# A DLRM-style recommender on one core: four late tables in two chunks instead of eight in four, in the last step

## The chip, the cores and the metric

The kernel runs on one core of one Trainium2 chip. The metric is the time on the device of one execution, in microseconds, taken by the median of several runs. All arithmetic is in float32.

## The reference

The batch has 2048 samples, each with 13 dense features and one index into each of 26 tables of 12,500 rows of 64 floats.

```python
x = relu(dense @ Wb0 + bb0)          # 13 -> 512
x = relu(x @ Wb1 + bb1)              # -> 256
d = relu(x @ Wb2 + bb2)              # -> 64
sp = emb[arange(26)[None, :], sparse_idx]
T = concatenate([sp, d[:, None, :]], axis=1)      # 27 vectors of 64 per sample
Z = einsum('bnd,bmd->bnm', T, T)
inter = Z[:, li, lj]                 # the 351 pairs below the diagonal
h = concatenate([d, inter], axis=1)
h = relu(h @ Wt0 + bt0)              # 415 -> 512
h = relu(h @ Wt1 + bt1)              # -> 256
p = sigmoid(h @ Wt2 + bt2)
```

## The kernel before, in words

The batch is worked off in 8 steps of 256 samples. A step is 128 columns `c` with two samples (halves `h`) each, and it is taken in two units `u` of 64 columns. The bottom layers run first; steps 1 to 6 are a loop for TensorE (L795), written out for VectorE; the last step has code of its own on every engine (`last_step`).

**Fetching the rows.** Of the 26 tables, 25 are gathered by GpSimd with indirect DMAs of 128 rows of 256 bytes (`gather`, L440). Table 25 (`FETCHED`) is fetched row by row: SP issues 128 single-row DMAs a step for half 0 (L399) and ScalarE's queue as many for half 1 (L878), each with its address in a register; four times a step the addresses are loaded from SBUF (`load_places`, L343). `keep_pace` (L365) holds both queues behind GpSimd's gathers.

**The last step's gathers.** Tables are taken in pairs, unit 0 first: `gather_pairs(0, r)` for six runs, then `gather_pairs(1, r)` for the first four runs (tables 0 to 15) of unit 1 (L472). The eight tables 16 to 23 of unit 1 are the *late* ones (`LATE`, `LATE_N`). Their rows come in four chunks `l` of 16 columns (`CHUNKED`), two halves each: 8 x 128 rows. GpSimd gathers seven of the eight (L475 to L478). The eighth, chunk `COPIED_L` = 2, half `COPIED_H` = 0, is fetched by SP with 128 single-row DMAs (L407) after all its fetches of table 25. The other 19 vectors of unit 1 (tables 0 to 15, table 24, the fetched one, and `d`) are *early* (`EARLY`).

**From rows to features.** TensorE turns rows into columns (`turn_last` L524, `turn_late` L541: a transposition by matmul into `ps_turn`). ScalarE moves half 0 and VectorE half 1 of a turn into `vecs_st` (stationary) and `vecs_mv` (moving) (`spread_last`, `spread_late`). TensorE multiplies the vectors of each column among themselves: `gram_early(b)` (L590) has 32 matmuls with 19-column weights and 38 moving columns; `gram_chunk(l)` (L600) has 16 with 32-column weights and the chunk's late vectors, 16 moving columns. A float32 matmul is two records in the trace. VectorE transposes the early products in 32 x 32 blocks (`turn_early`, L974), ScalarE picks the pairs (`pack`, L820): 171 early pairs. TensorE turns these in two tiles (`turn_feat_last`, L617), ScalarE moves them to `feat_t` (`move_feat`, L825), and TensorE adds them to the first top layer (`top_0_early(m)`, two matmuls for each of the four blocks `m` of 128). The late products are transposed by VectorE (`stand_late`, L964), turned in two tiles (`turn_late_feat`, L624), moved by ScalarE and VectorE, one tile each (`move_late`), and added with two matmuls a block (`top_0_late`, L639). Then come `top_1_sum` (L694), `logit` (L1009) and the sigmoid (L888).

**What sets the order.** Every engine runs its instructions in the order in which the code emits them; semaphores hold them back. `turn_late(l)` waits for its chunk's rows: `late_landed[l]`, and for the chunk that SP fetches also all 128 of `late_fetch_landed` (L544 to L546). `stay_busy(n)` (L612) are `n` matmuls of 256 columns whose result is used by nobody. TensorE's order is that of `last_step`; from `turn_last(10)` on it is

```python
turn_last(10); stay_busy(2); turn_last(11); stay_busy(1)
gram_early(0); turn_late(0); gram_early(1); gram_chunk(0); stay_busy(1)
turn_feat_last(); turn_late(1); top_0_early(0); top_0_early(1)
gram_chunk(1); turn_late(2); top_0_early(2); turn_late(3); top_0_early(3)
gram_chunk(2); gram_chunk(3); stay_busy(1)
turn_late_feat()
for m in range(T0 // P): top_0_late(m)
top_1_sum(i, 1)
```

(written here with semicolons; in the code it stands one call a line, L762 to L786).

## Time and profile before

| | |
|---|---|
| median of 3 runs | 863.91 us (863.19 to 867.28) |
| the profiled execution, its own time | 863.44 us |
| its span, first to last instruction | 861.7 us |
| TensorE busy (matmul) | 313.1 us, 36% |
| VectorE busy | 252.3 us, 29% |
| ScalarE busy | 19.3 us, 2% |
| GpSimd busy | 380.1 us, 44% |
| granted TensorE clock, mean | 0.626 |
| DMA, mean over the span | 21 GB/s, 20761 packets |

The profile is one execution, taken by the hardware profiler. Engines: PE is TensorE's matmul side, PEld its weight loads, DVE VectorE, ACT ScalarE, POOL GpSimd, SP SyncE; a name with a q (SPq, ACTq) is that engine's instruction queue, here its issuing of DMAs. A timeline row has the start in us, the length in us (from the first to the last of the x instructions merged in it), engine, line, operation, what is written and read, the shape, and in brackets how long the engine was idle before and what released it; "issue" means that the profile shows nothing that it waited for. A granted clock of 1.00 is 2.4 GHz, 0.50 is 1.2 GHz.

### The profile page before, as it was taken

The numbers are of one execution on the slowest core, as the hardware profiler recorded it, in microseconds if no ns is written. First come the engines' busy times: TensorE is split into PE (matmuls) and PEld (weight loads), VectorE is DVE, ScalarE is ACT, GpSimd is POOL, SyncE is SP. The second block draws the span as 40 slices with busy tenths as digits, with TensorE's granted clock in tenths as the row PEclk, the third lists the DMA queues.
The fourth block names the chain that finished last, engine by engine and source line by source line (L and its number), as shares of the span: only waits on it lengthen the run. The fifth ranks groups of instructions, "written<-read, shape, count | busy, mean of one in ns | idle before, by whom it ended". The sixth has DMA issues, their size and how long they took to land.

```text
span 861.7 us, 12006 instructions
## 1 busy us (share of the span) xinstructions
PE 313.1 (36%) x3235; PEld 225.9 (26%) x3235; DVE 252.3 (29%) x412; ACT 19.3 (2%) x46; POOL 380.1 (44%) x408
## 2 busy tenths in 40 slices
PE   4519441173013720174113720163113611045724
PEld 1203210072012610163002610162012611035613
DVE  6015342062222531052321631052321722032311
ACT  0000000000000000000000000000000000002211
POOL 7772561616643463706643463706733335710000
PEclk9759685576555855557555855576555855558676
DMA  7430230302321131302321132302311011100000
GB/s 192 26 27 11 21 25 4 26 6 23 25 16 15 15 24 14 27 3 26 23 16 15 14 23 14 28 3 25 25 14 16 14 14 19 27 7 1 3 3 1
DMA packets 20761, 17.88 MB, mean 21 GB/s; under 512 B 11987, under 2 KB 13276, under 8 KB 20697
## 3 DMA queue, kind: packets, MB, share of 16 engines
q0 software_dynamic: 12800, 13.10, 18.5%
q1 hardware_dynamic: 5178, 3.76, 1.5%
q10 hardware_dynamic: 2732, 0.51, 0.3%
q14 instruction: 41, 0.34, 0.2%
q8 instruction: 10, 0.16, 0.1%
HBM read 17.33 MB, written 0.01 MB: 20 GB/s over the span
## 4 chain that ended last, share of the span: by engine, by line
SPq 46%; issue 39%; PE 9%; DVE 2%; POOL 2%; DMA 1%; ACT 1%; another core or an unknown queue 0%; ACTq 0%; DVEq 0%
SPq L399 40%; SPq L343 6%; PE ps_gram L565 2%; POOL rows L441 2%; PE ps_t L681 1%; PE ps_t L702 1%; PE ps_feat L681 1%; DVE gram_s L985 1%; PE ps_gram L585 1%; DMA fetched<-in_emb 0%; DVE vecs_mv L949 0%; PE ps_turn L538 0%; DVE gram_s L987 0%; PE ps_t L692 0%
## 5 line engine op out<-in xcount | busy, mean ns | idle before, releaser
L441 POOL DMA_INDIRECT rows<-in_emb,idx_row x399 | 377.2, 945 | 376.7 <-PE ps_turn L516 238.3
L565 PE MATMUL ps_gram<-vecs_mv,vecs_st 128*32 128x54 f32 x1792 | 68.1, 293 | 183.7 <-issue 148.2
L565 PEld LDWEIGHTS ps_gram<-vecs_mv,vecs_st 128*32 128x32 f32 x1792 | 52.2, 169 | 201.0 <-issue 161.3
L516 PE MATMUL ps_turn<-ident,rows 128*128 128x128 f32 x182 | 32.8, 321 | 195.2 <-DVE rows L943 177.6
L949 DVE COPY vecs_mv<-ps_turn 64x512 f32<-64x512 f32 (+1 forms) x98 | 96.5, 985 | 0.7
L985 DVE STREAM_TRANSPOSE gram_s<-ps_gram 128x864 f32<-128x864 f32 x15 | 16.2, 1083 | 215.3 <-PE ps_gram L565 212.1
L516 PEld LDWEIGHTS ps_turn<-ident,rows 128*128 128x128 f32 x182 | 24.1, 163 | 204.9 <-issue 190.0
L702 PE MATMUL ps_t<-wt_sb,ht_t 128*128 128x256 f32 x128 | 44.0, 493 | 67.7 <-issue 46.1
L949 DVE COPY vecs_st<-ps_turn 128x512 f32<-128x512 f32 (+1 forms) x49 | 47.4, 967 | 13.6 <-issue 5.0
L702 PEld LDWEIGHTS ps_t<-wt_sb,ht_t 128*128 128x128 f32 x128 | 28.6, 240 | 84.3 <-issue 53.6
L943 DVE COPY rows<-fetched 128x128 f32<-128x128 f32 x8 | 1.8, 226 | 154.6 <-DMA fetched<-in_emb 154.6
L494 PE MATMUL ps_t<-hb,wb_sb 128*128 128x512 f32 x64 | 33.8, 689 | 21.7 <-issue 21.7
L681 PE MATMUL ps_t<-feat_t,wt_sb 117*128 117x128 f32 x180 | 32.7, 331 | 0.2 <-ACT feat_t L825 0.2
L681 PEld LDWEIGHTS ps_t<-feat_t,wt_sb 117*128 117x128 f32 x180 | 29.8, 245 | 0.4 <-ACT feat_t L825 0.4
L681 PE MATMUL ps_feat<-feat_t,wt_sb 117*128 117x128 f32 x180 | 27.0, 290 | 0.0
L681 PEld LDWEIGHTS ps_feat<-feat_t,wt_sb 117*128 117x128 f32 x180 | 25.0, 210 | 0.0
L494 PEld LDWEIGHTS ps_t<-hb,wb_sb 128*128 128x128 f32 x64 | 14.0, 226 | 41.4 <-issue 41.4
L804 ACT ACTIVATE vecs_st<-ps_turn 64x256 f32<-64x256 f32 (+1 forms) x13 | 7.0, 542 | 785.0 <-PE ps_turn L538 785.0
L1002 DVE TENSOR_SCALAR ht_t<-ps_t 128x256 f32<-128x256 f32 x12 | 5.1, 425 | 62.1 <-remote 47.0
L1006 DVE TENSOR_SCALAR ht_t<-ps_feat 128x256 f32<-128x256 f32 x16 | 6.8, 423 | 41.6 <-remote 26.8
L663 PE MATMUL ps_feat<-ident,feat 128*117 128x128 f32 x45 | 12.4, 401 | 15.8 <-DVE feat L993 13.9
L675 PE MATMUL ps_t<-d_t,wt_sb 65*128 65x128 f32 x60 | 14.2, 326 | 0.0
(99 smaller groups left out, 260.8 us busy)
## 6 DMA issues: line engine op xcount, KB each, us to landing
fetched<-in_emb ACTq DMA_DIRECT2D x1024, 0.2 KB
fetched<-in_emb SPq DMA_DIRECT2D x1024, 0.2 KB
rows<-in_emb,idx_row POOLq DMA_INDIRECT x399
rows<-in_emb SPq DMA_DIRECT2D x128, 0.2 KB
wt_sb<-in_wt SPq DMA_DIRECT2D x1, 1024.0 KB
wb_sb<-in_wb SPq DMA_DIRECT2D x1, 512.0 KB
wt_early_sb<-in_wt_early SPq DMA_DIRECT2D x1, 512.0 KB
wt_late_sb<-in_wt_late SPq DMA_DIRECT2D x1, 512.0 KB
```

Source lines behind the costliest of these rows:

```text
L343: _, places = nc.values_load_multi_w_load_instructions(fetch_at[h * PARTS + q:h * PARTS + q + 1, i * PART:(i + 1) * PART], engines=(engine ...
L399: sp.dma_start(landing(i, 0, q * PART + j), emb_bytes[bass.ds(places[j], ROW_BYTES)])\
L441: nc.gpsimd.indirect_dma_start(to, None, emb_rows, bass.IndirectOffsetOnAxis(idx_row[:, c:c + 1], 0)).then_inc(landed, 16)
L494: summed = nc.tensor.matmul((ps_t0, ps_t1)[m][:, :], wb1_sb[:, k, m * P:(m + 1) * P], hb0[:, k, :], start=(k == 0), stop=(k == B0 // P - 1))
L516: turned = nc.tensor.transpose(ps_turn[r % 2][:, j, :], rows[:, first + j, :], ident[:, :])
L565: summed = nc.tensor.matmul(ps_gram[32 * v:32 * v + 32, b, g * 2 * VECS:(g + 1) * 2 * VECS], vecs_st[:, c, :], vecs_mv[:, c, :, :].rearran ...
L663: turned = nc.tensor.transpose(ps_feat[u][0:PAIR_ROWS, k, :], feat[:, u, k * PAIR_ROWS:(k + 1) * PAIR_ROWS], ident[:, :])
L675: nc.tensor.matmul(top_0_blocks(u, m // 2)[:, m % 2, :], wt0_sb[0:D_ROWS, PAIR_TILES, m * P:(m + 1) * P], d_t[:, u, :], start=True, stop=F ...
L681: summed = nc.tensor.matmul(top_0_blocks(u, m // 2)[:, m % 2, :], wt0_sb[0:PAIR_ROWS, k, m * P:(m + 1) * P], feat_t[:, u, k, :], start=Fal ...
L702: summed = nc.tensor.matmul(ps_t1[:, 0:T1], ht0_t[:, k, :], wt1_sb[:, k, :], start=False, stop=(k == T0 // P - 1))
L949: moved = nc.vector.tensor_copy(to, source)
L985: nc.vector.transpose(gram_s[u][:, 0:VECS * SLOTS], unit_products(VECS)).then_inc(gram_turned, 1)
```

## The change

Four tables (20 to 23) of unit 1 are late instead of eight (16 to 23), in two chunks of 32 columns instead of four of 16; with unit 1's 64 columns and two samples in each, that is 4 x 128 late rows. GpSimd gathers three of the four; SP fetches chunk `COPIED_L` = 0, half 0. The fifth run of pairs of unit 1 (tables 16 to 19) is gathered and turned as early (`EARLY_RUNS` = 5, `LAST_NR` = 13). The early vectors become 23 and their pairs 253, in tiles of 127 and 126. The early products have 23-column weights and 46 moving columns; a chunk's products are 32 matmuls of 8 moving columns. The late pairs fill one tile of 128 instead of two. The second tile of the early features is turned into `ps_gram` and moved by VectorE (`move_early`), the first by ScalarE; the late tile is moved half by ScalarE and half by VectorE. The base indices of the late tables are written by four memsets where a table of eight memsets was transposed and copied. The order of `last_step` changes on TensorE, ScalarE and VectorE. Line numbers with the new kernel are lower by up to 7.

The core of the diff:

```diff
-LATE = 4 * HEAD
-LATE_N = 8
-CHUNKED = 4
+LATE_N = 4
+LATE = FETCHED - 1 - LATE_N
+EARLY_RUNS = LATE // 4
+CHUNKED = 2
 CHUNK_C = 64 // CHUNKED
-COPIED_L, COPIED_H = 2, 0
+COPIED_L, COPIED_H = 0, 0
...
             def gram_chunk(l):
 
                 wait_spread(LAST_NR + l)
-                gh, b = divmod(l, 2)
-                for g in range(4 * gh, 4 * gh + 4):
+                for g in range(HALF // 2):
...
             def turn_feat_last():
 
                 pe.wait_ge(feat_packed, STEPS * 2)
...
+                (lo, mid), (_, hi) = EARLY_TILES
+                nc.tensor.transpose(ps_feat[1][0:mid - lo, 0, :], feat[:, 1, lo:mid], ident[:, :]).then_inc(feat_turned, 1)
+                nc.tensor.transpose(early_block[0:hi - mid, :], feat[:, 1, mid:hi], ident[:, :]).then_inc(early_turned, 1)
...
                 if m == 0:
                     pe.wait_ge(late_low, 1)
...
+                    pe.wait_ge(late_high, 1)
+                summed = nc.tensor.matmul(top_0_blocks_last(m // 2)[:, m % 2, :], wt0_late_sb[:, 0, m * P:(m + 1) * P],
+                                          late_t[:, 0, :], start=False, stop=(m % 2 == 1))
...
                 turn_last(9)
                 top_1_bias(i, 1)
+                stay_busy(2)
                 turn_last(10)
-                stay_busy(2)
+                stay_busy(3)
                 turn_last(11)
+                stay_busy(3)
+                turn_last(12)
                 stay_busy(1)
                 gram_early(0)
                 turn_late(0)
                 gram_early(1)
                 gram_chunk(0)
-                stay_busy(1)
+                stay_busy(2)
+                turn_late(1)
+                gram_chunk(1)
                 turn_feat_last()
-                turn_late(1)
+                turn_late_feat()
                 top_0_early(0)
                 top_0_early(1)
-                gram_chunk(1)
-                turn_late(2)
+                top_0_late(0)
+                top_0_late(1)
                 top_0_early(2)
-                turn_late(3)
                 top_0_early(3)
-                gram_chunk(2)
-                gram_chunk(3)
-                stay_busy(1)
-                turn_late_feat()
-                for m in range(T0 // P):
-                    top_0_late(m)
+                top_0_late(2)
+                top_0_late(3)
                 top_1_sum(i, 1)
...
                 spread_last(11)
+                spread_last(12)
                 spread_late(0)
+                spread_late(1)
                 pack(i, 1)
                 move_feat(i, 1)
-                spread_late(1)
-                spread_late(2)
-                spread_late(3)
                 move_late()
...
+            def move_early():
+
+                dve.wait_ge(early_turned, 1)
+                n = EARLY_TILES[1][1] - EARLY_TILES[1][0]
+                nc.vector.tensor_copy(feat_t[0:n, 1, 1, :], early_block[0:n, :]).then_inc(early_moved, 1)
...
-            for n in range(4):
-                for jj in range(2):
-                    nc.vector.memset(late_tables[32 * n:32 * (n + 1), CHUNK_C * jj:CHUNK_C * (jj + 1)],
-                                     (LATE + 2 * n + jj) * VOCAB).then_inc(late_tables_ready, 1)
+            for n in range(LATE_N):
+                nc.vector.memset(idx_base[32 * n:32 * (n + 1), LATE_COLS:], (LATE + n) * VOCAB).then_inc(last_base_ready, 1)
```

TensorE's instructions before, from the first late turn's place on (`ps_turn` holds turned rows and the late products, L550 is `turn_late`, L585 `gram_early`, L608 `gram_chunk`, L615 a filler, L621 and L628 the turns of features, L636 and L646 the top layer):

```order
L585 MATMUL ps_gram<-vecs_mv,vecs_st 19x38 x32
L550 MATMUL ps_turn<-ident,rows 128x128
L585 MATMUL ps_gram<-vecs_mv,vecs_st 19x38 x32
L608 MATMUL ps_turn<-vecs_mv,vecs_st 32x16 x16
L615 MATMUL ps_feat<-wt_sb 128x256
L621 MATMUL ps_feat<-ident,feat 86x128
L621 MATMUL ps_feat<-ident,feat 85x128
L550 MATMUL ps_turn<-ident,rows 128x128
L636 MATMUL ps_t<-feat_t,wt_early_sb 128x128 x4
L608 MATMUL ps_turn<-vecs_mv,vecs_st 32x16 x16
L550 MATMUL ps_turn<-ident,rows 128x128
L636 MATMUL ps_feat<-feat_t,wt_early_sb 128x128 x2
```

The turn that waits for SP's rows, the third L550, is the last row here. The same place after the change (L549 is `turn_late`, L584 `gram_early`, L606 `gram_chunk`, L613 a filler, L619 and L620 the turns of the early features, L625 that of the late tile, L633 the top layer):

```order
L584 MATMUL ps_gram<-vecs_mv,vecs_st 23x46 x32
L549 MATMUL ps_turn<-ident,rows 128x128
L584 MATMUL ps_gram<-vecs_mv,vecs_st 23x46 x32
L606 MATMUL ps_turn<-vecs_mv,vecs_st 32x8 x32
L613 MATMUL ps_feat<-wt_sb 128x256 x2
L549 MATMUL ps_turn<-ident,rows 128x128
L606 MATMUL ps_turn<-vecs_mv,vecs_st 32x8 x32
L619 MATMUL ps_feat<-ident,feat 127x128
L620 MATMUL ps_gram<-ident,feat 126x128
L625 MATMUL ps_gram<-ident,late_s 128x128
L633 MATMUL ps_t<-feat_t,wt_early_sb 128x128 x4
L641 MATMUL ps_t<-late_t,wt_late_sb 128x128 x2
```

Now the turn that waits for SP's rows is the first L549; the early products' second half, both chunks, the turns of the features and the whole top layer stand behind it.

VectorE's instructions before, from the transposition of the early products on (L961 is `spread_late`, L977 and L979 `turn_early`, L968 `stand_late`, L972 `move_late`):

```order
L977 STREAM_TRANSPOSE gram_s<-ps_gram 128x608
L979 STREAM_TRANSPOSE gram_s<-ps_gram 128x288
L961 COPY vecs_st<-ps_turn 64x8x4x4
L961 COPY vecs_mv<-ps_turn 64x8x4x4
L961 COPY vecs_st<-ps_turn 64x8x4x4
L961 COPY vecs_mv<-ps_turn 64x8x4x4
L961 COPY vecs_st<-ps_turn 64x8x4x4
L961 COPY vecs_mv<-ps_turn 64x8x4x4
L968 STREAM_TRANSPOSE late_s<-ps_turn 128x256
L972 COPY late_t<-ps_gram 128x128
L1006 TENSOR_SCALAR ht_t<-ps_feat 128x256
```

After the change, from the first late spread on (L954 is `spread_late`, L976 and L978 `turn_early`, L961 `stand_late`, L971 `move_early`, L965 `move_late`):

```order
L954 COPY vecs_st<-ps_turn 64x4x4x8
L954 COPY vecs_mv<-ps_turn 64x4x4x8
L976 STREAM_TRANSPOSE gram_s<-ps_gram 128x736
L978 STREAM_TRANSPOSE gram_s<-ps_gram 128x352
L954 COPY vecs_st<-ps_turn 64x4x4x8
L954 COPY vecs_mv<-ps_turn 64x4x4x8
L961 STREAM_TRANSPOSE late_s<-ps_turn 128x128
L971 COPY feat_t<-ps_gram 126x128
L965 COPY late_t<-ps_gram 64x128
L1005 TENSOR_SCALAR ht_t<-ps_feat 128x256
L1011 SCALAR_TENSOR_TENSOR ht_w,logits<-ps_t,wt_sb 128x256
```

Two pairs of spreads less stand there, and the move of the second early tile is new.

## Rows read from the trace of the kernel before

**Rows 1.** Timeline of SP's queue: start us, us, queue line op out<-in xcount.

```profile
9.41 787.68 SPq L399 DMA_DIRECT2D fetched<-in_emb  x1024
...
799.35 48.59 SPq L407 DMA_DIRECT2D rows<-in_emb  x128
```

**Rows 2.** Waits of SP's queue: total us, times, longest us.

```profile
SPq L343 <- PE ps_turn L538: 2.0, 1, 2.0
...
SPq L343 <- DMA rows<-in_emb,idx_row: 1.6, 1, 1.6
```

**Rows 3.** Timeline, last 110 us: start us, us, engine line op xcount [idle before <-releaser].

```profile
756.78 0.94 POOL L441 DMA_INDIRECT rows<-in_emb,idx_row  x1 [0.30 <-issue]
...
763.24 1.79 PE L565 MATMUL ps_gram<-vecs_mv,vecs_st 128*32 128x54 f32 x66 [1.16 <-issue]
...
798.40 0.66 PE L538 MATMUL ps_turn<-ident,rows 128*128 128x128 f32 x2 [10.01 <-issue]
...
848.95 0.45 PE L550 MATMUL ps_turn<-ident,rows 128*128 128x128 f32 x1 [23.28 <-issue]
```

**Rows 4.** Timeline, the program's start.

```profile
2.61 0.18 DVE L1105 TENSOR_SCALAR idx_base<-idx_base 64x48 int32<-64x48 int32 x1 [0.53 <-POOL idx_base L424]
...
5.62 0.97 SPq L390 DMA_DIRECT2D wt_late_sb<-in_wt_late  x1
...
6.63 0.56 SPq L391 DMA_DIRECT2D wt_sb<-in_wt  x1
```

**Rows 5.** Stretches: length, busy PE, PEld, DVE, ACT, POOL (x), granted clock, DMA, GB/s.

```profile
849.00:850.00 1.00, 1.00 (x5) 1.00 (x6) 0.56 (x2) 0.56 (x2) 0.00 (x0) 0.50 0.00 0
...
856.00:857.00 1.00, 1.00 (x10) 1.00 (x10) 0.00 (x0) 0.38 (x1) 0.00 (x0) 0.92 0.00 0
```

**Rows 6.** Timeline, small products at half and at full clock.

```profile
800.35 3.11 PE L585 MATMUL ps_gram<-vecs_mv,vecs_st 128*32 128x54 f32 x128 [1.28 <-ACT vecs_mv L804]
...
819.71 0.76 PE L585 MATMUL ps_gram<-vecs_mv,vecs_st 128*19 128x38 f32 x64 [0.35 <-ACT vecs_mv L804]
```

**Rows 7.** Timeline of the tail.

```profile
850.05 0.42 PE L550 MATMUL ps_turn<-ident,rows 128*128 128x128 f32 x1
...
851.25 1.06 PE L608 MATMUL ps_turn<-vecs_mv,vecs_st 128*32 128x16 f32 x64
...
852.24 1.22 PE L615 MATMUL ps_feat<-wt_sb 128*128 128x256 f32 x2
...
853.25 0.42 PE L628 MATMUL ps_feat<-ident,late_s 128*128 128x128 f32 x1
...
853.92 0.29 DVE L972 COPY late_t<-ps_gram 128x128 f32<-128x128 f32 x1 [1.10 <-PE ps_gram L628]
...
854.25 2.06 PE L646 MATMUL ps_t<-late_t,wt_late_sb 128*128 128x128 f32 x8 [0.37 <-ACT late_t L815]
...
855.91 1.09 PEld L646 LDWEIGHTS ps_feat<-late_t,wt_late_sb 128*128 128x128 f32 x8
...
857.04 1.89 PE L702 MATMUL ps_t<-wt_sb,ht_t 128*128 128x256 f32 x8
```

**Rows 8.** Groups by shape, 798 to 862 us: line, shapes xcount | busy us, mean ns | idle before.

```profile
L985 DVE STREAM_TRANSPOSE gram_s<-ps_gram 128x864 f32<-128x864 f32 x1 | 1.1, 1083 | 3.3 <-PE ps_gram L585 3.3
...
L820 ACT ACTIVATE feat<-gram_s 128x351 f32<-128x351 f32 x1 | 0.8, 830 | 5.0 <-DVE gram_s L987 5.0
```

**Rows 9.** Timeline, top layer at full clock.

```profile
783.24 0.39 PE L675 MATMUL ps_feat<-d_t,wt_sb 65*128 65x128 f32 x2
...
784.13 0.39 PE L675 MATMUL ps_feat<-d_t,wt_sb 65*128 65x128 f32 x2
```

**Rows 10.** Stretches in which the clock rose before; columns as in rows 5.

```profile
770.00:772.00 2.00, 0.72 (x3) 0.41 (x2) 2.00 (x4) 0.00 (x0) 0.00 (x0) 0.80 0.01 1
...
811.00:812.00 1.00, 1.00 (x7) 1.00 (x6) 0.60 (x2) 0.96 (x3) 0.00 (x0) 0.61 0.00 0
```

**Rows 11.** Timeline, a matmul of the step before the last.

```profile
745.73 0.25 PE L565 MATMUL ps_gram<-vecs_mv,vecs_st 128*32 128x54 f32 x1 [2.55 <-issue]
```

66 lines of the change are left out of this document (25 added, 41 removed).

## The prediction

> **What bounds the kernel now.** I read the queue of SyncE (SP) first, then its waits, then the timeline of the last 110 us with the granted clock beside it. The program's end hangs on one queue. SP issues 1024 single-row DMAs of the fetched table from 9.41 to 797.09 us; right behind them come the 128 row DMAs that bring one half of one late chunk, from 799.35 to 847.94 us [rows 1]. Its list of waits holds 1.6 and 2.0 us in all before its address loads (L343) [rows 2], out of 790: it is busy issuing. GpSimd has issued its last gather by 757.7 us [rows 3], so every other late row has long been asked for when SP comes to its 128.
>
> TensorE does all that it can do without those rows, then stands idle for 23.28 us, and turns the chunk (L550, `turn_late(2)`) at 848.95 us [rows 3]. From there to the end of the span are **12.75 us**; I call this stretch the tail. Only two things can move the time: when SP's 128 rows are there, and how long the tail behind them is. Whatever is done between 800 and 848 us is covered by the 23 us of idle TensorE.
>
> **The change, part by part.**
>
> *SP and GpSimd.* After the change SP still issues 1024 + 128 row DMAs. GpSimd issues four gathers more for the fifth early run (L449) and four fewer late ones (three instead of seven): 399 as before. Nothing moves past anything on either queue before SP's last DMA, and SP's rate when it is alone is that of [rows 1], 48.59 us for 128. I take the landing as unchanged: 0.
>
> *Start.* VectorE loses eight memsets, a transpose and a copy, and gets four small memsets. They are covered: right behind them VectorE idles 0.53 us for GpSimd's iota, until 2.61 us [rows 4]. The late weights shrink from 512 to 256 KB; that DMA takes SP 0.97 us to issue, while the equally large one behind it takes 0.56 us [rows 4]. So SP may start its fetches between 0 and 0.5 us (half of 0.97) sooner, or not at all sooner, since the size doesn't explain these two. I take 0 and keep 0.5 us for the low end.
>
> *Where the SP rows are consumed.* This is the edit that counts. Before, SP's chunk is the third of four (`COPIED_L` 2); now it is the first of two (`COPIED_L` 0). Since TensorE runs in program order, everything behind `turn_late(0)` waits for 848.95 us: the second half of the early products, both chunks, two groups of fillers, the early features' turns and all four blocks of the top layer. Of that, the old order had the early products, two chunks, the features' turn and two blocks done before the wait. What goes away: top-layer products of the late tile fall from two a block to one, and the chunks' turns from four to two.
>
> The new tail, counted from TensorE's start at 848.95 us; the clock is at 0.50 there (1.2 GHz) [rows 5]:
> 1. `turn_late(0)` is one pass of 128 columns, 0.2 us (half of the 0.415 of step 6). `gram_early(1)`: 32 matmuls of 46 columns. At this clock 64 of 54 columns (128 records, two passes each) take 3.11 us [rows 6], 48.6 ns each; by columns 41.4 ns, x32 = 1.32. Now 1.55 us.
> 2. `gram_chunk(0)`: 32 matmuls of 8 columns on 32-column weights. The nearest row is the old pair of chunks, 32 matmuls of 16 columns in 1.06 us [rows 7]. Halving the columns might halve it (0.53), but 32 matmuls of 38 columns on 19-column weights take 0.76 us at full clock [rows 6], 1.52 by cycles at half of it: with less than half the columns the chunks' products came down by under a third. I take 1.06, the upper end. Now 2.6 us. The Trainium skill ("TensorE: Matmul & The Clock Gate", "Back-to-back issue gap") gives about 25 ns as floor for a matmul of up to 64 columns; by that, 64 passes a chunk would take 1.6 us, and both chunks 1.1 us more in the sum. The trace has 1.06 us for 64 passes, so I keep the row.
> 3. `stay_busy(2)`: one filler takes 1.0 us (852.24 to 853.25) [rows 7], two about 1.85. Now 4.45 us. The rows of chunk 1 are long there, but its turn stands behind the fillers.
> 4. `turn_late(1)`, spread by ScalarE and VectorE, then the products: from turn (850.05) to products (851.25) the trace has 1.2 us [rows 7]. Now 5.7 us. `gram_chunk(1)` 1.06: now 6.75 us. Beside this VectorE turns the early products (1088 columns in two; 864 take 1.08 us [rows 8], so 1.4) from 1.6 to 3.0 us, and ScalarE packs 253 columns behind its second spread (351 take 0.83 [rows 8], so at most that), done by 6.4 us: covered.
> 5. Two turns of the early features and the move that VectorE now shares: the old pair of turns and moves took from 853.25 to 854.25, when the next matmul starts [rows 7], so 1.0 us. Now 7.7 us. The late tile's turn and its two half moves run beside it and are there for the third product.
> 6. Top layer: 4 blocks x 3 = 12 matmuls of 128 columns. Four take 1.66 us at 1.2 GHz (854.25 to 855.91 [rows 7]: 0.415 each); at 2.4 GHz four take 0.89 us (783.24 to 784.13 [rows 9]: 0.222 each).
> 7. From the first `top_1` matmul to the end of the span: 857.04 to 861.7 us, 4.66 us at full clock [rows 7].
>
> **The clock decides between the ends.** In the old tail it rose 7.2 us after the start: the stretch 856 to 857 us shows 0.92, so it was half for 0.16 us of it [rows 5]. Two earlier restarts from 0.50 took longer: products began at full pace at 763.24 and the stretch 770 to 772 has 0.80 (half the clock for 40% of it, full for 60%: risen at 770.8), 7.6 us later; turns began at 798.40 and the stretch 811 to 812 has 0.61, risen at 811.8, 13.4 us later [rows 3, 10]. If it rises at 7.2 us again, the tail is 7.7 + 12 x 0.222 + 4.66 = 15.0 us, 2.3 more than now. At 9.4 us, the mean of the three: 1.7 us hold four matmuls at the low clock, eight remain, 7.7 + 1.7 + 1.75 + 4.66 = 15.8 us, **3.0 more** (3.05, rounded down). At 13.4 us: 7.7 + 4.98 + 4.66 + 0.3 = 17.6, 4.9 more. I take the middle one, since the new tail has a hole of nearly a microsecond at step 4, and its products with few columns lie where the old tail had top-layer matmuls.
>
> **Sum.** The profiled execution took 863.44 us (span 861.7, and 1.74 around it); 863.44 + 0 + 3.0 = **866.4 us**. The median of the runs, 863.91, is 0.5 us above that execution, and one of them was 867.28; I add nothing for it. 0.5% (4.3 us) is about what a measurement of this kernel can tell from no change, so my forecast is a loss too small to be sure of.
>
> **Rivals.**
>
> *A, slower: the clock stays low to the end.* One mechanism, in steps 3 to 7 of the tail: TensorE waits twice for ScalarE and VectorE, does turns and products with few columns, and the clock doesn't rise before `top_1`. Then the top layer takes 12 x 0.415 = 4.98 us and the four `top_1` matmuls twice their 1.66 us: 7.7 + 4.98 + 4.66 + 1.66 = 19.0, 6.2 more, **869.6 us**. It decides (over 868.2) from a rise later than about 13.4 us. For it: the restart at 798.40, 13.4 us with products and turns in it [rows 10]. Against: the restart at 763.24 had gaps as well and rose after 7.6 us. The Trainium skill ("TensorE: Matmul & The Clock Gate", "Part 4: PE-mode transpose") says that turns by TensorE don't count as busy for the clock, which speaks for this rival: it would keep the new tail's five turns out of the account. No row here separates turns from the rest. Chance 0.13.
>
> *B, no change: SP ends sooner.* The shorter weight load lets SP start up to 0.5 us earlier and its rate varies from run to run (863.19 to 867.28); 1.5 to 3 us less on SP cancel the longer tail: about **863.5 us**. For it: SP sets everything up to 848 us, so each microsecond there counts in full. Against: nothing but the 0.97 us of one DMA gets cheaper. Chance 0.10. Beyond that, a shift of SP of over 7 us would make it faster (857 us); the known edits give no such shift: 0.03.
>
> *C, slower: TensorE's instructions come slowly in the tail.* Between 743 and 763 us single matmuls stand 2.55 us apart with no wait behind them [rows 11]. The new tail has over twice the instructions of the old behind its wait, all of them after a long idle time. Two such gaps cost 5.1 us on top of 3.0: **871.5 us**. Against: the trace has them only while GpSimd or ScalarE issue DMAs too, and from 800 to 826 us, with SP alone issuing, 128 records go through in 3.11 us [rows 6]. Chance 0.04.
>
> **How the numbers follow.** The forecast (tail 2.3 to 4.9 longer, 865.7 to 868.3) has 0.70. It lies within 0.5% of before but for its last tenth of a microsecond. Faster by over 0.5%: 0.03. Slower: A 0.13, C 0.04 and nothing from the forecast's edge: 0.17. The same: 0.80. The range for 8 in 10 goes from 863.5 (B's value) to 869.7 us (just above A's); what it leaves out is C, part of B and the shift of SP, and run-to-run scatter at both ends.
>
> **What the new profile would show.** SP's last row DMA still ends near 848 us, and TensorE's idle time before `turn_late(0)` is still over 20 us, with `gram_early(1)`, all 64 chunk matmuls, the features' turns and the whole top layer behind it. Steps 1 to 5 reach 7.7 us after the restart, the top layer takes 2.7 to 5 us by the clock of its stretch, and 4.7 us remain. I am wrong if SP's last DMA moves by more than a microsecond, if the restart isn't bound to SP's rows at all, or if the tail is under 14 us: then the chunks or the fillers were over-priced, or an order that I read as binding was not.

## The result and the profile after

| | before | changed |
|---|---|---|
| median, 22 runs each | 864.93 us (861.40 to 870.74) | 869.62 us (864.07 to 874.67) |
| the profiled execution, its own time | 863.44 us | 869.74 us |
| its span | 861.7 us | 867.7 us |
| granted TensorE clock, mean | 0.626 | 0.62 |

The ratio of the changed kernel to the one before is 1.0047, with a 95% interval of 1.0027 to 1.0067: **slower by 2 to 6 us**, and just under the 0.5% that I had set as the edge of what can be told from no change. The forecast was 866.4 us; the range ended at 869.7, so the measured 869.62 is inside by 0.1 us.

The profiled execution took 6.3 us more than that of before, 863.44 against 869.74. It divides in three, each of them a difference of two single executions. SP's queue, in the timeline of the changed kernel (start us, us, queue line operation, xcount):

```profile
9.26 789.19 SPq L398 DMA_DIRECT2D fetched<-in_emb  x1024
800.71 48.56 SPq L406 DMA_DIRECT2D rows<-in_emb  x128
```

The last row DMA has been issued by 849.27 us where before it was 847.94 [rows 1], and TensorE's restart moves with it, from 848.95 [rows 3] to 850.29 us: **+1.34 us**. The tail behind the restart grows from 12.75 to 867.7 - 850.29 = 17.41 us: **+4.66 us**. The rest, +0.3 us, lies around the span. The tail, TensorE and what it waits for (start us, us, engine, line, operation, xcount, idle before and its releaser):

```profile
824.64 0.85 PE L584 MATMUL ps_gram<-vecs_mv,vecs_st 128*23 128x46 f32 x64 [0.35 <-ACT vecs_mv L798]
...
850.29 0.45 PE L549 MATMUL ps_turn<-ident,rows 128*128 128x128 f32 x1 [24.80 <-DMA rows<-in_emb]
...
850.67 1.44 PE L584 MATMUL ps_gram<-vecs_mv,vecs_st 128*23 128x46 f32 x64
...
851.90 1.03 PE L606 MATMUL ps_turn<-vecs_mv,vecs_st 128*32 128x8 f32 x64
...
852.85 2.08 PE L613 MATMUL ps_feat<-wt_sb 128*128 128x256 f32 x4
...
854.72 0.42 PE L549 MATMUL ps_turn<-ident,rows 128*128 128x128 f32 x1
...
855.94 1.04 PE L606 MATMUL ps_turn<-vecs_mv,vecs_st 128*32 128x8 f32 x64 [0.80 <-DVE vecs_mv L954]
...
858.19 2.04 PE L633 MATMUL ps_t<-feat_t,wt_early_sb 127*128 127x128 f32 x8 [0.26 <-DVE feat_t L971]
...
860.88 1.90 PE L633 MATMUL ps_feat<-feat_t,wt_early_sb 127*128 127x128 f32 x8
...
863.06 1.89 PE L696 MATMUL ps_t<-wt_sb,ht_t 128*128 128x256 f32 x8
```

The restart waits for SP's rows (`DMA rows<-in_emb`) for 24.80 us, as before for 23.28 [rows 3]; the first half of the early products, at 824.64, is the last thing done ahead of it. Everything the diff put behind `turn_late(0)` stands behind 850.29: the second half of the early products (L584), the first chunk (L606, 64 records), the two fillers (L613), the second chunk's turn (L549 at 854.72), its products, the turns of the features, and the top layer from 858.19 to 863.06. The granted clock in that stretch (length, busy PE, PEld, DVE, ACT, POOL, clock, DMA share, GB/s):

```profile
852.00:854.00 2.00, 2.00 (x75) 1.80 (x65) 1.38 (x2) 0.00 (x0) 0.00 (x0) 0.50 0.03 8
...
862.00:863.00 1.00, 1.00 (x8) 1.00 (x8) 0.00 (x0) 0.00 (x0) 0.00 (x0) 0.68 0.00 0
863.00:864.00 1.00, 1.00 (x8) 0.89 (x7) 0.42 (x1) 0.00 (x0) 0.00 (x0) 1.00 0.00 0
```

It stays at 0.50 (1.2 GHz) through nearly all of the top layer. The stretch 862 to 863 us has 0.68: full speed for 0.36 us of it, so the clock rose at 862.64, **12.35 us after the restart**, 0.4 us ahead of `top_1`. Before, it rose 7.2 us after [rows 5].

### The profile page after: what moved, and what is told of

It reads as the page before. It is cut to its first block, busy times and chain, and to the rows that moved or that the text cites. A ratio compares the mean times of both kernels' runs of the same rounds, so it can differ in the third digit from the quotient of the medians.

```text
span 867.7 us, 12002 instructions
## 1 busy us (share of the span) xinstructions
PE 318.1 (37%) x3238; PEld 229.5 (26%) x3238; DVE 252.8 (29%) x405; ACT 19.0 (2%) x44; POOL 379.8 (44%) x408
## 4 chain that ended last, share of the span: by engine, by line
SPq 56%; issue 36%; PE 4%; POOL 2%; DVE 1%; DMA 1%; another core or an unknown queue 0%; ACT 0%; ACTq 0%; DVEq 0%
SPq L398 45%; SPq L341 7%; SPq L406 4%; POOL rows L440 2%; PE ps_gram L564 1%; PE ps_turn L515 0%; DVE gram_s L984 0%; PE ps_t L633 0%; PE ps_feat L613 0%; PE ps_t L675 0%; PE ps_turn L606 0%; PE ps_t L696 0%; DMA idx_raw<-in_idx 0%; PE ps_feat L633 0%
## 5 line engine op out<-in xcount | busy, mean ns | idle before, releaser
L564 PE MATMUL ps_gram<-vecs_mv,vecs_st 128*32 128x54 f32 x1792 | 67.4, 292 | 185.8 <-issue 157.7
L493 PE MATMUL ps_t<-hb,wb_sb 128*128 128x512 f32 x64 | 35.7, 720 | 21.6 <-issue 21.6
```

Source lines behind the costliest of these rows:

```text
L493: summed = nc.tensor.matmul((ps_t0, ps_t1)[m][:, :], wb1_sb[:, k, m * P:(m + 1) * P], hb0[:, k, :], start=(k == 0), stop=(k == B0 // P - 1))
L564: summed = nc.tensor.matmul(ps_gram[32 * v:32 * v + 32, b, g * 2 * VECS:(g + 1) * 2 * VECS], vecs_st[:, c, :], vecs_mv[:, c, :, :].rearran ...
```

## The experiments

Two theories stand against each other for the loss, and a third for its size.

- **Order.** SP's rows set the restart; they are now needed by the first late turn, so that more work lies behind them. Then moving SP's rows to the last chunk takes the loss away, and moving them to the first chunk in the *old* kernel makes it.
- **SP is later.** The new program makes SP end later (the +1.34 us), by its loads or by what other engines do beside it. Then the restart is later in every variant of the new program.
- **Clock.** Of the longer tail most is the low clock: the same instructions at full clock would take no longer than the old tail.

The experiments ran on four chips. Each kernel is compared with the kernel before on its own chip; the kernel before took, by the median, 865.43 us on the first (experiments 1 to 3 and the 50 fillers of 4), 868.27 us on the second (5 and 6), 862.81 us on the third (7 and the 60 fillers of 4), and 517.88 us on the fourth, to which the last experiment belongs. The changed kernel itself was not run again on them. A ratio is followed by its 95% interval; a tail is read from one profiled execution.

### 1. SP's rows in the last chunk

```diff
-COPIED_L, COPIED_H = 0, 0
+COPIED_L, COPIED_H = 1, 0
```

> The changed kernel with one number changed: SP's 128 single-row DMAs now bring half 0 of chunk 1, the last, instead of chunk 0. Theory 1 (the loss is the work that stands behind the turn that waits for SP's rows): the first half of the tail (steps 1 to 3 of the prediction, 4.5 us) moves before the wait; from TensorE's restart remain turn to products 1.2, products 1.06, turns and moves 1.0, top layer 12 x 0.415 = 5.0, and 4.66 to 6.3 for the rest: 12.9 to 14.6 us instead of 17.4, time 3 to 4.5 us under the changed kernel. Theory 2 (the new program makes SP's queue end later, 850.3 instead of 849.0 us): the restart stays at 850.3 or later and is at most 1.3 us of the loss; seen here in the restart time alone.

Measured: 864.40 us, ratio 0.9988 [0.9961, 1.0016]. The timeline behind the restart:

```profile
850.60 0.45 PE L549 MATMUL ps_turn<-ident,rows 128*128 128x128 f32 x1 [22.07 <-issue]
...
851.84 1.04 PE L606 MATMUL ps_turn<-vecs_mv,vecs_st 128*32 128x8 f32 x64 [0.80 <-DVE vecs_mv L954]
...
854.09 2.05 PE L633 MATMUL ps_t<-feat_t,wt_early_sb 127*128 127x128 f32 x8 [0.26 <-DVE feat_t L971]
...
857.93 1.89 PE L696 MATMUL ps_t<-wt_sb,ht_t 128*128 128x256 f32 x8
```

The products of the second chunk start 1.2 us after the restart and `top_1` 7.3 us after it, where the changed kernel took 12.8. The tail is 862.6 - 850.60 = 12.0 us, less than the 12.9 to 14.6 expected, because the clock rose about 5.8 us after the restart (the stretch 856 to 857 us has 0.81) and the top layer with it took 3.84 us instead of the 5.0 at the low clock. The loss is gone with one digit changed, and the restart, 850.60, is no earlier than in the changed kernel, 850.29: **order holds, and the later SP is not what made the loss.**

### 2. The kernel before, with SP's rows in its first chunk

```diff
-COPIED_L, COPIED_H = 2, 0
+COPIED_L, COPIED_H = 0, 0
```

> The kernel before with one number changed: SP's 128 rows belong to chunk 0 instead of chunk 2 (the place that the change gives them), nothing else. Theory 1: the whole rest of the unit stands behind SP's rows as in the changed kernel; the tail grows from 12.75 to about 20 us (four chunks, two turns more and 16 late top-layer matmuls instead of four), span about 869, slower than before by about 0.8% and no better than the changed kernel. Theory 2 (the place of SP's rows does not matter, the sizes of the late tile do): time as before, 865.

Measured: 869.97 us, ratio 1.0061 [1.0028, 1.0094]. The restart and the start of `top_1` in its timeline:

```profile
853.00 0.45 PE L550 MATMUL ps_turn<-ident,rows 128*128 128x128 f32 x1 [28.20 <-DMA rows<-in_emb]
...
867.09 1.89 PE L702 MATMUL ps_t<-wt_sb,ht_t 128*128 128x256 f32 x8
```

The span ends at 871.7: a tail of 18.7 us against some 20 expected, with the rise of the clock 11.4 us after the restart (the stretch 864 to 865 us has 0.78). (The 16 late top-layer matmuls of the expectation are 16 records, so 8 matmuls.) This one edit of the old kernel costs about as much as the whole change: 1.3 us more in the profiled tail, with intervals of the ratios that overlap. What the change does besides (two turns and four top-layer products fewer behind the restart) gave no more than that back.

### 3. Without the two fillers of the tail

```diff
                 gram_chunk(0)
-                stay_busy(2)
                 turn_late(1)
```

> The changed kernel without the two fillers between the products of chunk 0 and the turn of chunk 1. Theory 1: they are plain work in the tail; it shrinks by their 1.85 us to about 15.5. Theory 3 in its strong form (the fillers are what brings the clock up in time): without them the clock rises after the top layer, top_1 takes 1.7 us more, and the tail stays at about 17.2 us.

Measured: 869.03 us, ratio 1.0036 [1.0006, 1.0066]; the profiled tail is 868.2 - 852.96 = 15.24 us, as expected.

```profile
852.96 0.45 PE L549 MATMUL ps_turn<-ident,rows 128*128 128x128 f32 x1 [26.27 <-DMA rows<-in_emb]
```

The tail is 2.2 us shorter than the changed kernel's. The fillers themselves are 1.9 us of that, as priced in step 3; the rest lies in what is beside them, above all the clock, which rose 9.6 us after the restart (0.71 in 862 to 863) and so gave the top layer 0.5 us. The strong form of the third theory, that the fillers bring the clock up, is refuted: it rose ahead of `top_1` without them. In the medians the gain (869.03, on a chip where the kernel before takes 865.43) is too small to tell from none.

### 4. TensorE kept at work through the wait

```diff
                 gram_early(0)
+                stay_busy(50)
                 turn_late(0)
```

> The changed kernel with 50 filler matmuls (0.42 us each at full clock, some 21 us) between gram_early(0) and turn_late(0), where TensorE stands idle for 24.8 us. They end some 3 us before SP's rows land, so they delay nothing. Theory 3 (part of the new tail is the low clock): the clock is 1.00 at the restart and stays there; the steps of the tail at full clock are 0.1 + 0.85 + 0.9 + 0.9 + 1.2 + 0.9 + 0.8 + 2.7 + 4.7 = 13.0 us instead of 17.4; time 4.4 us under the changed kernel. Rival: the steps wait for ScalarE and VectorE or are bound by instruction rate, and the tail shrinks by under 2 us.

Measured: 866.93 us, ratio 1.0025 [0.9999, 1.0050]; the tail is 862.5 - 846.58 = 15.92 us, not 13.0.

```profile
846.58 0.30 PE L549 MATMUL ps_turn<-ident,rows 128*128 128x128 f32 x1 [3.73 <-issue]
```

The stretches show the clock:

```profile
842.00:846.00 4.00, 0.85 (x4) 0.40 (x3) 0.00 (x0) 0.00 (x0) 0.00 (x0) 1.00 0.00 1
846.00:847.00 1.00, 0.42 (x18) 0.33 (x22) 0.08 (x1) 0.08 (x1) 0.00 (x0) 1.00 0.00 1
847.00:848.00 1.00, 1.00 (x81) 1.00 (x73) 0.55 (x2) 0.56 (x2) 0.00 (x0) 0.57 0.05 16
...
850.00:851.00 1.00, 0.87 (x3) 0.34 (x2) 0.09 (x1) 0.09 (x1) 0.00 (x0) 0.72 0.00 0
...
854.00:855.00 1.00, 1.00 (x7) 1.00 (x7) 0.00 (x0) 0.00 (x0) 0.00 (x0) 0.50 0.00 0
857.00:858.00 1.00, 1.00 (x9) 1.00 (x8) 0.00 (x0) 0.00 (x0) 0.00 (x0) 0.81 0.00 0
```

The fillers ended at 842.85 and TensorE stood for 3.73 us. The clock was still 1.00 at the restart (846.58), fell to 0.50 at 847.1 (0.57 in that microsecond: full speed for 0.14 of it), was back at 850.6, fell again at 854.0, in the top layer, and rose once more at 857.4. **Missed, by the clock**, which fell 0.5 us behind a gap of 3.73 us ahead of the tail. If the gap is the reason, the fillers have to reach the restart:

```diff
                 gram_early(0)
+                stay_busy(60)
                 turn_late(0)
```

> The run with the filled wait again, with 60 fillers instead of 50 (25.3 us): they then end within a microsecond or two of the landing of SP's rows, in place of 3.7 us before it. Theory 3 (the idle gap before the restart is what lets the clock fall): the clock stays at 1.00 through the first products, and the tail is 13 to 14 us instead of 15.9. Rival (products with few columns and the waits of steps 3 and 4 let it fall, as it did a second time 7.4 us after the restart there): the clock is at 0.50 again within the tail, which stays at 15 us or more.

Measured: 865.77 us, ratio 1.0037 [1.0016, 1.0057]. Of its timeline:

```profile
826.00 26.17 PE L613 MATMUL ps_feat<-wt_sb 128*128 128x256 f32 x120
...
852.32 0.30 PE L549 MATMUL ps_turn<-ident,rows 128*128 128x128 f32 x1 [0.16 <-issue]
...
853.46 0.71 PE L606 MATMUL ps_turn<-vecs_mv,vecs_st 128*32 128x8 f32 x64
...
857.74 1.13 PE L633 MATMUL ps_t<-feat_t,wt_early_sb 127*128 127x128 f32 x8
...
860.49 1.89 PE L696 MATMUL ps_t<-wt_sb,ht_t 128*128 128x256 f32 x8
```

and of its stretches

```profile
852.00:854.00 2.00, 1.79 (x130) 1.43 (x129) 1.17 (x3) 0.66 (x2) 0.00 (x0) 1.00 0.00 0
...
858.00:860.00 2.00, 2.00 (x20) 2.00 (x20) 0.00 (x0) 0.38 (x1) 0.00 (x0) 1.00 0.00 0
```

The clock did not fall this time. The same instructions as in the changed kernel, at 1.00 throughout, take 865.1 - 852.32 = **12.78 us instead of 17.41**: the low clock is 4.6 us of the new tail, the third theory. The top layer's step is 857.74 to 860.49, 2.75 us where it was 4.87. But the median doesn't follow: the tail is as long as that of before and the kernel still takes 0.37% more, 3.2 us. In the profiled execution (866.91 us) the restart is at 852.32, 3.4 us later than before [rows 3], and the fillers did not hold it up: it came 1.05 us after SP's last DMA (851.27), as in the others (1.0 to 1.3 us). In other executions they may. They took 26.17 us from `gram_early(0)` on, and the wait that they fill differs from one execution to the next: 24.80 us in the changed kernel, about 22.9 with 50 fillers, 26.27 without the tail's fillers. Against the first two they would end 1.4 and 3.3 us late; that is an estimate from three profiles. Where SP is later still they end too soon, and the clock may fall as in the run above. Neither was tested, and the 3 us are open.

### 5. SP's single rows taken away

One more gather of 128 rows by GpSimd takes the place of SP's 128 DMAs; in the changed kernel and in the one before.

```diff
-            sp.wait_ge(rows_turned, STEPS * NR)
-            for jj in range(4):
-                places = load_places(mybir.EngineType.SP, 0, jj, STEPS)
...
-                    if (l, h) != (COPIED_L, COPIED_H):
-                        gather(LATE_COLS + 2 * l + h, late_rows(l)[:, h * DIM:(h + 1) * DIM], late_landed[l])
+                    gather(LATE_COLS + 2 * l + h, late_rows(l)[:, h * DIM:(h + 1) * DIM], late_landed[l])
...
-                if l == COPIED_L:
-                    pe.wait_ge(late_landed[l], 16)
-                    pe.wait_ge(late_fetch_landed, 16 * P)
-                else:
-                    pe.wait_ge(late_landed[l], 32)
+                pe.wait_ge(late_landed[l], 32)
```

> The changed kernel, with SP's 128 single-row DMAs taken out and the fourth late gather issued by GpSimd like the other three (one indirect DMA, 1.25 us of GpSimd's time, done near 759 us). Theory 1 (the time is SP's 1152 single-row DMAs plus the tail): the 24.8 us of idle TensorE before turn_late(0) vanish and the tail runs on at the clock that TensorE has by then; the profiled timeline has gram_early(0) at 824.6 us, and 13.7 us of tail at full clock follow: about 840 us, 28 less. Rival (late rows are slow on GpSimd's queue too): TensorE waits again at turn_late(0), time over 850.

> The kernel before with the same edit: no single-row DMAs for the late chunk, all eight late gathers on GpSimd. Theory 1: TensorE goes on at 825.7 us instead of waiting to 849, and 10.8 us of work remain at full clock: about 838 us. The difference between this and the run before tells what the change is worth where SP's rows are not in the way: by this count nothing or a loss of 1 to 2 us, since all rows are there and only the amount of work counts (54 against 38 columns of early products and fillers, 12 against 24 top-layer matmuls).

Measured: 846.19 us, ratio 0.9737 [0.9681, 0.9793], for the changed kernel so edited, and 843.88 us, 0.9731 [0.9689, 0.9774], for the one before. With the late wait gone, no difference between the two orders is shown: the medians are 2.3 us apart with four executions each, and the intervals are 4 to 5 us wide to either side. SP's rows took 48.6 us; about half of that was hidden behind TensorE's own work. Against the kernel before, in which TensorE had stood for 23.28 us [rows 3], the medians are 22.1 and 24.4 us lower.

Both ended some 6 us later than expected (846.19 against 840, 843.88 against 838), on a chip where the kernel before takes 868.27 us, 3.3 more than in the result above. In the profile of the old order the clock is 1.00 through the tail; that of the changed one shows a pause of TensorE in the middle of the first chunk's products, and from 832.4 us on a low clock (0.54 in the stretch 832 to 834 us):

```profile
828.13 0.53 PE L593 MATMUL ps_turn<-vecs_mv,vecs_st 128*32 128x8 f32 x42
...
829.98 0.37 PE L593 MATMUL ps_turn<-vecs_mv,vecs_st 128*32 128x8 f32 x22 [1.32 <-issue]
```

Nothing in the profile is waited for there: rival C's kind of gap, in the tail, at half of the 2.55 us of [rows 11]. It comes when SP's row DMAs (until 801.4 us) and GpSimd's gathers (until 760.0 us) have long been issued.

### 6. No single-row DMAs at all

Table 25 too is gathered by GpSimd, two gathers a step (416 gathers where experiment 5 has 400); SP and ScalarE issue no rows any more.

```diff
+            def gather_fetched(i):
+
+                if i == 0:
+                    pool.wait_ge(idx_ready, 3)
+                for h in range(2):
+                    gather(FETCH_COLS + 2 * i + h, fetched[:, i, h * DIM:(h + 1) * DIM], fetch_landed[h][i])
...
-                dve.wait_ge(fetch_landed[h][i], 16 * P)
+                dve.wait_ge(fetch_landed[h][i], 16)
```

> The changed kernel with no single-row DMAs at all: table 25 too is gathered by GpSimd, two indirect DMAs a step, and the late chunk as well (416 gathers instead of 399, 2176 single-row DMAs less). Theory 1 carried on (SP's queue sets the pace from the first step to the last): GpSimd becomes the bound with 416 x 1.25 us = 520 us from 4 us on, the last rows are there near 527 us, and a tail of about 12 us follows: some 540 us, 38% less. Rival (GpSimd's gathers are held back by buffers, since TensorE's turns or VectorE's moves take the steps' time): 600 us or more, with GpSimd's waits for rows_turned staying where they are, near 370 us in all.

> The kernel before with the same edit as the run before. Here the rows of the last chunk come last for real, one gather after another, so the two layouts of the late tables meet the case that they differ in: how much is left to do after the last gather. Expected: within 2 us of the run before, about 540 us; the old order has one chunk of 16 products, 16 late top-layer matmuls and a filler behind it, the new one 32 products, the early features and 12 matmuls.

Measured: 778.75 us, ratio 0.8988 [0.8949, 0.9028], and 778.44 us, 0.8960 [0.8913, 0.9008], again with no difference to be seen between the orders. Both are a tenth faster than the kernel before; both missed the 540 us by far. I had taken GpSimd's own time, 416 x 1.25 us, for the next bound. The waits of the changed kernel so edited (engine, line, releaser: total us, times, longest):

```profile
PE ps_gram L553 <- issue: 154.0, 146, 3.7
POOL rows L425 <- PE ps_turn L508: 148.0, 8, 20.6
```

GpSimd waits 148 us for TensorE's turns, and TensorE 154 us for nothing that the profile shows, in 146 pauses among its products. A stretch of its timeline:

```profile
324.67 1.73 PE L553 MATMUL ps_gram<-vecs_mv,vecs_st 128*32 128x54 f32 x51 [12.69 <-DVE vecs_mv L923]
...
326.74 0.42 PE L553 MATMUL ps_gram<-vecs_mv,vecs_st 128*32 128x54 f32 x5 [0.34 <-issue]
...
328.92 0.42 PE L553 MATMUL ps_gram<-vecs_mv,vecs_st 128*32 128x54 f32 x5 [1.03 <-issue]
```

51 records run in 1.73 us, then five at a time with pauses up to 1.03 us. The kernel before has the same, `PE ps_gram L565 <- issue`, 148.2 us in 101 pauses. So the single-row DMAs of the other two engines are not needed for the pauses: they stay without them. GpSimd's gathers remain, and the pauses end with them:

```profile
701.18 0.94 POOL L425 DMA_INDIRECT rows<-in_emb,idx_row  x1 [0.30 <-issue]
...
705.49 0.25 PE L553 MATMUL ps_gram<-vecs_mv,vecs_st 128*32 128x54 f32 x1 [2.55 <-issue]
...
709.00 1.49 PE L553 MATMUL ps_gram<-vecs_mv,vecs_st 128*32 128x54 f32 x53 [0.40 <-issue]
...
712.16 3.11 PE L553 MATMUL ps_gram<-vecs_mv,vecs_st 128*32 128x54 f32 x128 [1.67 <-DVE gram_s L967]
```

The row at 701.18 is the last gather. The last pause of this group of products stands before 709.00, 6.9 us after that gather's end, and the next 128 records of the same shape go through in 3.11 us in one piece. In the kernel before it is the same: the last gather ends at 757.7, the last such pause before 763.24 [rows 3]. That the gathers make the pauses is not shown: no run took them away, and experiment 8 has them without the pauses, on another chip. The pauses do not account for all of the 240 us between 778 and 540: the chain that ended last in this run is 24% `issue`, 24% TensorE, 23% VectorE, and 27% unattributed.

### 7. The early half of the top layer ahead of the last rows

SP's rows in the last chunk, and the early features turned, moved and added to all four blocks before the turn that waits.

```diff
-COPIED_L, COPIED_H = 0, 0
+COPIED_L, COPIED_H = 1, 0
...
-                turn_late(1)
-                gram_chunk(1)
                 turn_feat_last()
+                for m in range(T0 // P):
+                    top_0_early(m)
+                turn_late(1)
+                gram_chunk(1)
                 turn_late_feat()
...
+                for m in range(T0 // P):
+                    top_0_late(m)
```

(The same on ScalarE and VectorE: `pack`, `move_feat` and `move_early` ahead of `spread_late(1)`.)

> The changed kernel with SP's rows in the last chunk (as in the first run) and with the early features' turns, their moves and all their top-layer products put ahead of the turn of that chunk on TensorE, ScalarE and VectorE. Theory 1: only the last chunk's turn, 32 products, one turn of the late tile, 4 top-layer matmuls and top_1 are left behind SP's rows: 3.5 us to the first late product, 4 x 0.415 = 1.7, then 4.66 (6.3 if the clock is still low): 9.9 to 11.5 us of tail instead of 17.4 in the changed kernel and 12.0 with the chunk alone moved. The time should be 1 to 3 us under the kernel before. Rival: with so little work behind the restart the clock stays low to the end, and what is saved in work is lost in clock: tail about 11.5, no gain against the first run.

Measured: 862.03 us, ratio 0.9988 [0.9961, 1.0016]; the tail is 862.6 - 850.77 = 11.83 us, what the expectation's rival had said.

```profile
850.77 0.45 PE L549 MATMUL ps_turn<-ident,rows 128*128 128x128 f32 x1 [14.57 <-issue]
...
854.44 1.19 PE L641 MATMUL ps_t<-late_t,wt_late_sb 128*128 128x128 f32 x4 [0.48 <-DVE late_t L961]
...
856.28 3.62 PE L696 MATMUL ps_t<-wt_sb,ht_t 128*128 128x256 f32 x8
```

`top_1` starts 5.5 us after the restart, 1.8 sooner than in experiment 1, and loses it again: the clock didn't rise before 859.9 us, so that `top_1` took 3.62 us instead of the 1.89 of 863.06 above. Less work behind the wait, and all but its end at the low clock. This profiled execution is a long one (866.74 us). Over all twelve the span has a median of 858.9 us against 861.0 of the kernel before, 2.1 us less, but the time around the span has grown from 1.8 to 3.1 us; what lies in that time the profile doesn't show, and it takes back more than half of the gain.

The same order with everything gathered:

> The changed kernel with every row gathered by GpSimd, and the early-first order of this call. In the run with every row gathered (778.75 us) GpSimd issued its last gather at 701 us, and TensorE was still some 30 us from its late work: the order of the late work has nothing to wait for there. Theory: the time is TensorE's own sequence, so the reordering gives at most 1 us (the early matmuls fill the gap in which TensorE waits for the spreads of chunk 1): 777 to 779 us. Rival (the order was costing waits there too): 775 or less.

Measured: 782.47 us as the median of 6 runs from 769.92 to 787.41, beside 862.81 us of the kernel before. Experiment 6 had 778.75 beside 868.27. The order brings nothing that can be seen where no late transfer stands in front of it, but a spread of 17 us could hide a few microseconds.

### 8. Both: early half first, and TensorE kept at work

The edits of experiment 7, and with them:

```diff
                     top_0_early(m)
+                stay_busy(26)
                 turn_late(1)
```

> The early-first order with 26 fillers in the 14.6 us in which TensorE waits for SP's rows there (some at half clock until it rises, the rest 0.42 us each: 12.5 to 14 us, so that they end before the rows land). Theory 3: the tail then runs at full clock: 1.1 us from turn to products, 0.7 for them, 1.1 to the first late product, 4 x 0.222, 4.66: about 8.5 us instead of 11.8 in the early-first run and 12.75 in the kernel before; time 4 us under the kernel before. Rival, from the last filled run (whose tail was 4.6 us shorter than the changed kernel's in the profile and whose median gained less): the fillers cost about 3 us elsewhere in executions that aren't profiled, and the time is only 1 us under the kernel before.

This run fell on a chip where the kernel before takes 517.88 us (515.61 to 520.14). Measured: 532.86 us, ratio 1.0279 [1.0245, 1.0313]. SP's queue and the tail there:

```profile
9.26 437.80 SPq L398 DMA_DIRECT2D fetched<-in_emb  x1024
449.55 48.66 SPq L406 DMA_DIRECT2D rows<-in_emb  x128
```
```profile
506.56 0.50 PE L606 MATMUL ps_turn<-vecs_mv,vecs_st 128*32 128x8 f32 x22 [1.85 <-issue]
...
513.28 11.39 PE L613 MATMUL ps_feat<-wt_sb 128*128 128x256 f32 x52
...
524.51 0.27 PE L549 MATMUL ps_turn<-ident,rows 128*128 128x128 f32 x1
...
528.68 1.99 PE L696 MATMUL ps_t<-wt_sb,ht_t 128*128 128x256 f32 x8
```

The tail has about the length that was expected (8.5), 533.4 - 524.51 = 8.9 us at full clock. But SP's rows were there by 498.2 us, long before they were needed: here SP needs 437.8 us for the 1024 DMAs that take 789.2 on the other chips (0.43 us each against 0.77), while the 128 that it issues alone take the same 48.6. Of the 437.8 us, 33.4 are waits for GpSimd's gathers (`SPq L341 <- DMA rows<-in_emb,idx_row`; 0.8 us in the changed kernel's profile), so that 0.39 us each are left, nearly the 0.38 of the 128 alone. The page of the profile, its head and its chain:

```profile
PE 318.7 (60%) x3290; PEld 234.9 (44%) x3290; DVE 253.1 (47%) x405; ACT 19.3 (4%) x44; POOL 379.9 (71%) x408
...
POOL 52%; PE 20%; issue 19%; DMA 4%; DVE 3%; ACT 1%; POOLq 0%; DVEq 0%; ACTq 0%
...
L564 PE MATMUL ps_gram<-vecs_mv,vecs_st 128*32 128x54 f32 x1792 | 41.2, 275 | 30.1 <-DVE vecs_mv L939 16.1
```

GpSimd is busy for 71% of the span and 52% of the chain is its gathers; the products have 30.1 us of idle time before them in place of 185.8 in the changed kernel's profile, where 157.7 are `issue`. **The bound is another one**, and the 26 fillers, 11.39 us in the row at 513.28, fill no wait. Without them the kernel would take about 521.5 us by subtraction, still 3.6 more than before; that is an estimate, since without them the clock could have been another. The change as it was made wasn't run on such a chip, so its worth there is open.

The row at 506.56 has a pause of 1.85 us at the same record (the 43rd of the first chunk's 64) at which experiment 5 paused for 1.32 us. Experiments 1 (1.37 us), 6 (the changed kernel so edited, 1.79 us) and 7 (1.58 us, and 1.32 us with everything gathered) have it at that record too: all six runs of the changed program in which no wait of 20 us and no added fillers stand just ahead of those products. In the changed kernel, where TensorE had stood for 25 us just ahead, it isn't there: those 64 records take 1.03 us in one piece. The old order has no such pause in its chunks' products, in experiments 5 and 6 either. So the change brings a pause of 1.3 to 1.9 us that isn't seen behind its own long wait and that comes once the wait is gone.

## Why the prediction was right in kind and at the edge in size

**What bounds the kernel: right.** SP's 1024 + 128 row DMAs set the restart in every run that kept them, on the chips of 865 us, and the time of the last 128 is the steadiest number of all (48.54 to 48.66 us in nine profiles, the chip of 518 us included).

**SP unchanged: right, but my test of it was too tight.** "I am wrong if SP's last DMA moves by more than a microsecond": it moved by 1.33. Yet over eight profiles with the same SP queue, before among them at 848.95, TensorE restarts anywhere from 846.58 to 853.00 us, the earliest with the new program and the latest with the old. So the 1.34 us are within the scatter of 1024 DMAs over 790 us, and no effect of the change on SP is shown. The saved half of the weight load (0.77 us of issue instead of 0.97) is lost in it: rival B didn't come about.

**Steps 1 to 5 and 7 of the tail: right.** Counted from the restart at 850.29:

| step | predicted | measured |
|---|---|---|
| 1. turn and early products | 1.55 | 1.6 (851.90) |
| 2. first chunk, 32 products in 64 records | 2.6 | 2.56 (852.85) |
| 3. two fillers | 4.45 | 4.4 (854.72) |
| 4. second turn, spread, second chunk | 6.75 | 6.6 (856.91, first feature turn) |
| 5. turns and moves of the features | 7.7 | 7.90 (858.19) |
| 6. top layer, 12 matmuls | 11.1 | 12.77 (863.06) |
| 7. `top_1` to the end | + 4.66 | + 4.64 |

The choice with the widest alternatives, 1.06 us for a chunk's 64 records whatever their columns, was right to 0.03 us: 1.03 and 1.04 us, 16 ns a record, with 8 columns in place of 16. By the 25 ns for each pass that the Trainium skill ("TensorE: Matmul & The Clock Gate", "Back-to-back issue gap") gives as the floor, the estimate would have been 1.6 us a chunk. The trace is below it at either clock: 16 ns a record at the low one, and at full clock 0.71 us for 64, 11 ns each (853.46 in the run with 60 fillers). These products write to four groups of 32 partitions in turn, which that section doesn't speak of.

**The term that was mis-sized is the sixth step, by its clock.** I took "9.4 us, the mean of the three" rises of the trace; it was 12.35 us. So the twelve matmuls of the top layer took 4.87 us and not 3.45, and the tail grew by 4.66 us and not 3.0. My upper end for it, a rise after 13.4 us and 4.9 us more, was nearly the truth. Rival A, the clock low through `top_1` too, came within 0.4 us of its beginning but didn't happen in this kernel; in experiment 7 it did, and its price for `top_1` (1.66 us more) was about right there: 3.62 against 1.89 us. I had said what speaks for a late rise (a hole at step 4, products with few columns) and then took the middle. The Trainium skill ("TensorE: Matmul & The Clock Gate", "Part 4: PE-mode transpose") says that turns by TensorE don't count as busy in the same way. The late rise would fit that, but no run here separates it: rises came 5.8, 9.1, 9.6, 11.4 and 12.35 us after a restart in programs with much the same kinds of work behind it.

**The median.** 864.93 + 4.66 = 869.6 us, against 869.62 measured. So close a fit is luck, with tails from single executions and an interval of 2 us to either side. The forecast started from 863.44, one execution that was 1.5 us below the median of 22; this and the 1.66 us of the clock are its whole error of 3.2 us. That the range held is luck too: the band of the forecast itself (865.7 to 868.3) was missed, and the range reached to 869.7 only to take in rival A's 869.6, which is what was measured, but not by A's mechanism. Over the experiments the sum holds within about 1 us: the profiled tail less 12.75 us beside what the ratio gives at 865 us (to be read with 2 to 3 us to either side) is

| kernel | tail less 12.75 us | by the ratio |
|---|---|---|
| changed | +4.66 | +4.1 |
| 1. SP's rows last | -0.75 | -1.0 |
| 2. before, SP's rows first | +5.95 | +5.3 |
| 3. no fillers in the tail | +2.5 | +3.1 |
| 4. 50 fillers | +3.2 | +2.2 |
| 7. early half first | -0.9 | -1.0 |
| 4. 60 fillers | 0.0 | +3.2 |

Only the last doesn't fit; it is the open one above.

**Rival C** had no place in the tail of this kernel: there is no `issue` pause between 850.29 and 863.06. Its mechanism exists, at 1.3 to 1.9 us (experiments 1 and 5 to 8). What I had held against it, that the trace has such gaps only while GpSimd or ScalarE issue DMAs too, is wrong for these: at 829 us in experiment 5 no engine issued any.

## What to carry to other kernels

Where a kernel's end hangs on one slow transfer, count what stands behind the instruction that waits for it, in program order, and have the slowest transfer wanted last: here one index was worth about 5 us in both kernels, and all the other edits together nothing that could be measured. Price the work behind a long wait at the low clock, up to its very end; filler work kept the clock up in the profiled tail only where it lasted until the wait was over, brought nothing in the medians that could be told from none, and costs its length where the transfer comes sooner, as it does on another chip. Before polishing the tail, ask what the slow queue is for: on the chips of 865 us, 128 single-row DMAs of 48.6 us replaced by one gather brought 22 to 24 us, some five times what the order was worth.

## What the runs showed of the hardware that I had not expected

- Two speeds of chip for one program, 862.8 to 868.3 us on three chips and 517.88 us on one, with the same 48.6 us for SP's 128 lone DMAs and the same 380 us of busy GpSimd. What differs is what runs beside gathers: SP's DMAs (0.77 us each against 0.39 without their waits) and TensorE's instruction stream (185.8 against 30.1 us idle before the products). Both could have one cause; no run here shows it.
- TensorE's `issue` pauses stay when SP and ScalarE issue no row DMAs at all (154.0 us in 146 pauses), and stop 6.9 us after GpSimd's last gather there and 5.5 us after it in the kernel before.
- The granted clock changed four times in 10.3 us (847.1 to 857.4, experiment 4), and it rose anywhere from 5.8 to 12.35 us after a restart in programs that differ by a few instructions.
- A pause of TensorE came at the same record of the same group in six different runs (experiments 1 and 5 to 8; 1.3 to 1.9 us), so at least some pauses belong to a place in the program.
